# Edge scores of an attention layer: linear term from the value projection, gather in two float32r products, heads halved on POOL, projections first

## The reference

```python
Xq = (H @ W_lin.T).reshape(bt, n, h, dh)
Xv = (H @ W_val.T).reshape(bt, n, h, dh)
Qs, Kt = Xq[:, src], Xq[:, dst]
e = einsum('behd,hd->beh', leaky_relu(Qs + Kt, 0.2), a)
e = e + log(A0[src, dst] + EPS)[None, :, None]
attn = softmax of e over the edges that share src
Y = segment_sum(attn[..., None] * Xv[:, dst], src)
return Y.reshape(bt, n, d) @ W_out.T
```

## Time and profile before

| | |
|---|---|
| median of 3 runs | 1267.29 us (1266.42 to 1267.98) |
| profiled execution | 1267.61 us |
| its span, first to last instruction | 1265.7 us |
| mean granted TensorE clock | 0.995 |
| score stage (turns 0 to 15) | about 992 to 1142 us of the span |

### The profile page before, as it was taken

How to read it: one execution, slowest core, us unless ns; L and a number is a source line. 1 busy time by engine, 2 the same in 40 slices (tenths; PEclk the granted TensorE clock), 3 DMA queues, 4 the chain that set the end, 5 groups by cost and what they waited for, 6 DMA issues and landing times.

```text
span 1265.7 us, 22613 instructions
## 1 busy us (share of the span) xinstructions
PE 1226.4 (97%) x7334; PEld 1021.7 (81%) x7334; DVE 1012.4 (80%) x2032; ACT 871.6 (69%) x1657; POOL 335.3 (26%) x748
## 2 busy tenths in 40 slices
PE   8989989999999998999999999999999899999998
PEld 8989976653588886788879877988898777878998
DVE  6888859977678876988798879887876699987664
ACT  5666658868478877877787778777765577763332
POOL 6777730000176430000000000000000566653331
PEclk9999999999999999999999999999999999999999
DMA  8000000000211100000000000002100300001112
GB/s 310 2 1 2 2 1 0 0 1 0 100 68 66 66 34 1 1 1 1 1 1 1 1 1 1 1 1 84 51 1 1 134 1 1 2 1 47 71 68 83
DMA packets 14923, 38.22 MB, mean 30 GB/s; under 512 B 1904, under 2 KB 3952, under 8 KB 13808
## 3 DMA queue, kind: packets, MB, share of 16 engines
q1 hardware_dynamic: 14000, 36.60, 7.6%
q10 hardware_dynamic: 832, 0.46, 0.1%
HBM read 20.27 MB, written 16.78 MB: 29 GB/s over the span
## 4 chain that ended last, share of the span: by engine, by line
PE 53%; DVE 5%; ACT 2%; issue 1%; POOL 1%; POOLq 0%; DVEq 0%; ACTq 0%
PE bank L1108 7%; PE bank L1110 7%; PE bank L1109 7%; PE bank L1580 4%; PE bank L1123 4%; PE bank L1374 4%; PE bank L1119 4%; PE bank L1120 4%; PE bank L1362 4%; PE bank L1570 2%; PE bank L1588 2%; ACT gates L1138 1%; PE bank L1346 1%; PE bank L1264 1%; DVE Y L1193 1%
## 5 line engine op out<-in xcount | busy, mean ns | idle before, releaser
L1138 ACT ACTIVATE gates<-bank,lstm_bias 128x512 f32<-128x512 f32 (+1 forms) x504 | 301.9, 636 | 100.9 <-PE bank L1123 87.7
L170 ACT ACTIVATE l_h<-X,nmr,rstd 128x128 f32<-128x128 f32 (+1 forms) x512 | 210.0, 483 | 48.0 <-POOLq L164 31.0
L1108 PE MATMUL bank<-lstm_node_hi,Wih_hi 128*128 128x512 f32 (+1 forms) x408 | 149.4, 366 | 0.0
L1110 PE MATMUL bank<-lstm_node_lo,Wih_hi 128*128 128x512 f32 (+1 forms) x408 | 148.9, 365 | 0.0
L1109 PE MATMUL bank<-lstm_node_hi,Wih_lo 128*128 128x512 f32 (+1 forms) x408 | 148.8, 365 | 0.0
L138 POOL TENSOR_TENSOR l2r_sum<-l2r_st 128x8 f32<-128x8 f32 x16 | 4.2, 263 | 528.2 <-DVE l2r_st L112 528.2
L1119 PE MATMUL bank<-lstm_hid_hi,Whh_hi 128*128 128x512 f32 (+1 forms) x288 | 104.1, 361 | 3.9 <-DVE lstm_hid_hi L1198 3.8
L1123 PE MATMUL bank<-lstm_hid_lo,Whh_hi 128*128 128x512 f32 (+1 forms) x288 | 106.9, 371 | 0.0
L1120 PE MATMUL bank<-lstm_hid_hi,Whh_lo 128*128 128x512 f32 (+1 forms) x288 | 103.1, 358 | 0.0
L1143 ACT ACTIVATE gates<-lstm_cell 128x512 f32<-128x512 f32 (+1 forms) x144 | 83.7, 581 | 20.8 <-DVE lstm_cell L1185 20.4
L1110 PEld LDWEIGHTS bank<-lstm_node_lo,Wih_hi 128*128 128x128 f32 x408 | 77.1, 189 | 11.6
(11 more groups left out here) (248 smaller groups left out, 3301.7 us busy)
## 6 DMA issues: line engine op xcount, KB each, us to landing
x_spill<-X SPq DMA_DIRECT2D x32, 256.0 KB, 2.0
X<-x_spill SPq DMA_DIRECT2D x2, 4096.0 KB, 12.5
out<-X SPq DMA_DIRECT2D x32, 256.0 KB, 2.0
X<-in_x SPq DMA_DIRECT2D x6, 1024.0 KB, 15.3
X<-in_x SPq DMA_DIRECT2D x3, 512.0 KB, 8.1
w_raw<-in_WihT SPq DMA_DIRECT2D x1, 1024.0 KB, 5.5
w_raw<-in_WhhT SPq DMA_DIRECT2D x1, 1024.0 KB, 7.9
X<-in_x SPq DMA_DIRECT2D x2, 256.0 KB, 3.2
```

What stands on the lines that cost most here:

```text
L170: last = act.activation(h[:, j, :], k.X[:, bass.ds(b0, TB), :][:, j, :], ACT.Relu, bias=k.nmr[:, bass.ds(b0, TB)][:, j:j + 1], scale=k.rst ...
L1108: pe.matmul(out, hi, x_high, start=True, stop=False)
L1110: last = pe.matmul(out, hi, x_low, start=False, stop=it.step == 0)
L1138: act.activation(gate_of(it, g), k.bank[4 * s + g][:, 0:it.N], ACT.Tanh if g == GATE_G else ACT.Sigmoid, bias=k.lstm_bias[:, it.p - 1, g:g ...
```

## The change

- The linear term comes with the value projection. In the output stage of the second layer DVE builds `Wval`, 132 columns (in the place of the weights W1T, which are done with): the 128 of the value projection and four with the query weights times a_sign, summed by head. The value product of a tile then has 132 columns, and ACT copies the last four to `q_sums`. Qs, its POOL product and its DVE sum go.
- The gather is done with F32R operands: ACT rounds the queries to `q_hi`, DVE makes `q_lo = psQ - q_hi`, and PE adds two products for each half. `PT` becomes F32R.
- POOL `halve` adds the upper 16 features of each head in M to the lower 16, in place; DVE `sum_heads` sums those 16, and does so a turn later, behind the additions to X.
- PE does the query products of both slots first, then the value products of both. ACT does `normalise` of turn i+1, slot 0, ahead of the copies q_hi, and that of slot 1 at the end of its turn. DVE's statistics come behind q_lo.
- The PSUM banks are dealt out anew: a tile's values take two banks, one of them that of psT.

```diff
+            def value_projection():
+                W, H = e.Wval[:, :], k.HEADS
+                dve.tensor_tensor(W[:, 0:P], e.Wqv[:, 0:P], e.a_sign[:, :], ALU.mult).then_inc(joined, 1)
+                dve.wait_ge(joined, 1)
+                dve.tensor_reduce(W[:, P:P + H], W[:, 0:P].rearrange("p (x d) -> p x d", x=H), mybir.AxisListType.X,
+                                  ALU.add).then_inc(joined, 1)
+                dve.wait_ge(joined, 2)
+                dve.tensor_copy(W[:, 0:P], e.Wqv[:, P:2 * P]).then_inc(joined, 1)
+
             coef_dve(dve)
+            value_projection()
...
-        self.psR, self.psT, self.psQ, self.psV = (k.bank[n:n + 2] for n in (0, 2, 4, 6))
+        self.psR, self.psT, self.psQ, self.psV = ((k.bank[m], k.bank[n]) for m, n in ((0, 1), (3, 7), (4, 5), (2, 6)))
+        self.values = each(S, lambda s: k.psum[:, (2 + 4 * s) * TW:(4 + 4 * s) * TW].rearrange("p (b x) -> p b x", b=TB))
...
+    def halve(self, pool, i, s):
+        pool.wait_ge(self.R["M"][s], i + 1)
+        heads = self.M[s][:, :, :].rearrange("p c (x d) -> p (c x) d", d=self.k.DH)
+        first, second = heads[:, :, 0:self.k.DH // 2], heads[:, :, self.k.DH // 2:]
+        pool.tensor_tensor(out=first, in0=first, in1=second, op=ALU.add).then_inc(self.R["half"][s], 1)
+
+    def sum_heads(self, dve, i):
+        HW = TB * self.k.HEADS
+        for s in range(self.S):
+            t = i * self.S + s
+            dve.wait_ge(self.R["half"][s], i + 1)
+            dve.tensor_reduce(self.scores[:, :, t * HW:(t + 1) * HW],
+                              self.M[s][:, :, :].rearrange("p c (x d) -> p c x d", x=HW)[:, :, :, 0:self.k.DH // 2],
+                              mybir.AxisListType.X, ALU.add).then_inc(self.R["kept"][s], 1)
...
 on_pool
             for s in range(S):
-                if i:
-                    pool.wait_ge(R["lin"][s], i)
-                pool.wait_ge(R["Xq"][s], i + 1)
-                pool.tensor_tensor(out=Qs[s][:, :, :], in0=Xq[s][:, :, :],
-                                   in1=e.a_sign[:, :].unsqueeze(1).broadcast_to([P, TB, P]),
-                                   op=ALU.mult).then_inc(R["Qs"][s], 1)
+                self.halve(pool, i, s)
             if i + AHEAD < n_it:
                 ln.coefficients(pool, i + AHEAD)
...
 on_scalar
+            if i + 1 < n_it:
+                self.normalise(act, i + 1, 0)
             for s in range(S):
-                if i:
-                    act.wait_ge(R["Qs"][s], i)
                 act.wait_ge(R["Q"][s], i + 1)
-                act.activation(Xq[s][:, :, :], as_tile(psQ[s]), ACT.Copy).then_inc(R["Xq"][s], 1)
+                act.activation(q_hi[s][:, :, :], as_tile(psQ[s]), ACT.Copy).then_inc(R["hi"][s], 1)
+            for s in range(S):
+                t = i * S + s
                 act.wait_ge(R["V"][s], i + 1)
-                act.activation(Xv[:, rows(i, s), :], as_tile(psV[s]), ACT.Copy).then_inc(R["Xv"][s], 1)
-                if i + 1 < n_it:
-                    self.normalise(act, i + 1, s)
+                act.activation(Xv[:, rows(i, s), :], self.values[s][:, :, 0:P], ACT.Copy)
+                act.activation(e.q_sums[:, t * HW:(t + 1) * HW].rearrange("p (b x) -> p b x", b=TB),
+                               self.values[s][:, :, P:P + HEADS], ACT.Copy).then_inc(R["Xv"][s], 1)
+            if i + 1 < n_it:
+                self.normalise(act, i + 1, 1)
...
 on_tensor
-                for n, (ps, done) in enumerate(((psQ[s], R["Q"][s]), (psV[s], R["V"][s]))):
-                    for j in range(TB):
-                        last = pe.matmul(ps[:, j * P:(j + 1) * P], hT[s][:, j, :], e.Wqv[:, n * P:(n + 1) * P],
-                                         start=True, stop=True)
-                    last.then_inc(done, 1)
+                for j in range(TB):
+                    last = pe.matmul(psQ[s][:, j * P:(j + 1) * P], hT[s][:, j, :], e.Wqv[:, 0:P], start=True, stop=True)
+                last.then_inc(R["Q"][s], 1)
+            for s in range(S):
+                for j in range(TB):
+                    last = pe.matmul(self.values[s][:, j, 0:P + HEADS], hT[s][:, j, :], e.Wval[:, :], start=True, stop=True)
+                last.then_inc(R["V"][s], 1)
...
-                for c, (ps, free) in enumerate(((psQ[s], R["Xq"][s]), (psV[s], R["Xv"][s]))):
-                    pe.wait_ge(free, i + 1)
-                    pe.matmul(ps[:, :], e.PT[:, c * P:(c + 1) * P], Xq[s][:, :, :], start=True, stop=True).then_inc(R["G"][s], 1)
+                pe.wait_ge(R["lo"][s], i + 1)
+                for c, ps in enumerate((psQ[s], psV[s])):
+                    if c == 1:
+                        pe.wait_ge(R["Xv"][s], i + 1)
+                    pe.matmul(ps[:, :], e.PT[:, c * P:(c + 1) * P], q_hi[s][:, :, :], start=True, stop=False)
+                    pe.matmul(ps[:, :], e.PT[:, c * P:(c + 1) * P], q_lo[s][:, :, :], start=False, stop=True).then_inc(R["G"][s], 1)
...
 on_vector
             if i + AHEAD < n_it:
-                self.update(dve, i + AHEAD, tail_in)
+                self.add_residual(dve, i + AHEAD, tail_in)
+            if i:
+                self.sum_heads(dve, i - 1)
+            for s in range(S):
+                dve.wait_ge(R["hi"][s], i + 1)
+                dve.tensor_tensor(q_lo[s][:, :, :], as_tile(psQ[s]), q_hi[s][:, :, :].bitcast(F32),
+                                  ALU.subtract).then_inc(R["lo"][s], 1)
+            if i + AHEAD < n_it:
+                self.statistics(dve, i + AHEAD)
...
-            for s in range(S):
-                dve.wait_ge(R["M"][s], i + 1)
-                dve.tensor_reduce(scores[:, :, t * HW:(t + 1) * HW], M[s][:, :, :].rearrange("p c (x d) -> p c x d", x=HW),
-                                  mybir.AxisListType.X, ALU.add).then_inc(R["kept"][s], 1)
-            for s in range(S):
-                dve.wait_ge(R["Qs"][s], i + 1)
-                dve.tensor_reduce(e.q_sums[:, t * HW:(t + 1) * HW], Qs[s][:, :, :].rearrange("p b (x d) -> p (b x) d", x=HEADS),
-                                  mybir.AxisListType.X, ALU.add).then_inc(R["lin"][s], 1)
+        self.sum_heads(dve, n_it - 1)
...
-        self.psV, self.psY, self.psO = ((bank[2], bank[3]), (bank[4], bank[6])), (bank[0], bank[5]), bank[7]
+        self.psV, self.psY, self.psO = ((bank[3], bank[7]), (bank[4], bank[2])), (bank[0], bank[5]), bank[6]
```

More of the change, by code:

```diff
@@ L1239, in __init__ @@
         EC = k.E // P
-        at = lambda name, shape, offset: k.nc.alloc_sbuf_tensor_at(name, shape, F32, offset=offset)
+        at = lambda name, shape, offset, t=F32: k.nc.alloc_sbuf_tensor_at(name, shape, t, offset=offset)
         tile = 4 * TW
-        self.h, self.hT, self.Xq, self.Qs = (each(S, lambda s: at(f"l3_{n}{s}", [P, TB, P], x_at + (m * S + s) * tile))
-                                             for m, n in enumerate(("h", "hT", "Xq", "Qs")))
+        self.h, self.hT = (each(S, lambda s: at(f"l3_{n}{s}", [P, TB, P], x_at + (m * S + s) * tile))
+                           for m, n in enumerate(("h", "hT")))
+        self.q_hi, self.q_lo = (each(S, lambda s: at(f"l3_{n}{s}", [P, TB, P], x_at + (m * S + s) * tile, F32R))
+                                for m, n in ((2, "q_hi"), (3, "q_lo")))
         e.q_sums = at("q_sums", [P, k.B * k.HEADS], w_at)
@@ L1267, in update, with add_residual @@
     def update(self, dve, i, tail_in):
+        self.add_residual(dve, i, tail_in)
+        self.statistics(dve, i)
+    def add_residual(self, dve, i, tail_in):
         X, R = self.k.X, self.R
@@ L1274, in update, with statistics @@
             dve.tensor_tensor(xt, as_tile(self.psR[s]), xt, ALU.add).then_inc(R["updated"][s], 1)
+    def statistics(self, dve, i):
         for s in range(self.S):
-            dve.wait_ge(R["updated"][s], i + 1)
-            self.ln.stats(dve, X[:, self.rows(i, s), :], s, i)
+            dve.wait_ge(self.R["updated"][s], i + 1)
+            self.ln.stats(dve, self.k.X[:, self.rows(i, s), :], s, i)
+    def halve(self, pool, i, s):
[11 more added lines that the diff above has]
+                              mybir.AxisListType.X, ALU.add).then_inc(self.R["kept"][s], 1)
     def normalise(self, act, i, s):
@@ L1285, in on_pool @@
         EC, HEADS, HW = k.E // P, k.HEADS, TB * k.HEADS
-        h, hT, Xq, Qs, M, ln, rows = self.h, self.hT, self.Xq, self.Qs, self.M, self.ln, self.rows
+        h, hT, q_hi, q_lo, M, ln, rows = self.h, self.hT, self.q_hi, self.q_lo, self.M, self.ln, self.rows
         psT, psQ, psV = self.psT, self.psQ, self.psV
@@ L1354, in on_tensor @@
             for s in range(S):
-                if i == n_it - 1 and s == S - 1:
-                    at.sm.turn_back(pe, 0)
                 pe.wait_ge(R["hT"][s], i + 1)
@@ L1455, in linear_term @@
         for c in range(self.EC):
-            last = pe.matmul(self.first[:, c * P:(c + 1) * P], self.e.PT[:, c * P:(c + 1) * P],
+            last = pe.matmul(self.first[:, c * P:(c + 1) * P], self.e.PT[:, c * P:(c + 1) * P].bitcast(F32),
```

18 lines of the change are left out of this document (11 added, 7 removed).

## The result

1331.4 us (median of 5, 1331.2 to 1333.4) against 1268.0 for the kernel before on the same chip (median of 5, 1266.4 to 1269.4): 1.050 times the time [1.049, 1.052], 5% slower. Forecast was 1333, with 1318 to 1350 around it from its own terms and 1316 to 1352 with the rivals taken in. The profiled execution took 1331.8 with a span of 1330.1, 64.4 more than the span of before, so it accounts for the whole difference.

A forecast was written before the change was run, and what follows sets the result against it. PE and DVE were both taken as full at 8.79 us a turn before; after, a loop of waits. Terms 2.8 + 58.1 + 4.8 - 1.0 + 1.3 = 66 on 1267.3 gave 1333 us, range 1316 to 1352.

The forecast's parts named there:

- The closed loop M - halving - coefficients - normalise - q_hi - q_lo - M: Score stage, once a turn: the queue orders make each engine wait for the next, 13.26 us against 8.79, 4.47 more.
- neither waits for the other: Score stage of the kernel before: PE and DVE both fill the 8.79 us turn without waiting for each other.
- turn 0: First turn of the score stage: normalisation stands in front of q_hi, so its last M ends 2.8 us later.
- turn 14: Score stage: no statistics, but the linear-term addition, two transposes and a gather; about 13.4 us for 8.62, 4.8 later.
- turn 15: Last turn of the score stage: normalises nothing; softmax, reductions and q_lo take 4.63 us where 5.59 stood, 1.0 earlier.
- behind E(15): After the end of turn 15's last M: POOL's v_lo queues behind the last halving, delaying PE's gather; 1.3 us later.
- W: Output stage: three new DVE instructions, at most 1.2 us, counted as nothing, with 1.2 kept for the range.
- Busy time (a): Rival, score stage: no waiting, DVE's 7.74 us a turn decides, about 1252 us, faster; 5 in 100.
- The clock (b): Rival, score stage: PE idles, then gathers and projections run slow, 14.6 us a turn, about 1351 us; 8 in 100.
- The rule that the prediction took from the Trainium skill: A loop leaving PE idle long each round starts its products slow; here every turn's gathers would begin at 1.2 GHz.
- The halving (c): Rival, POOL in the score stage: halvings cost 2.5 us each, both on the path, 2.4 a turn, about 1366; 5 in 100.
- (d): Rival, score stage: some links of the path overlap and the stage loses little; 2 in 100.

The follow-up runs named there:

- the kernel with three turns of lead: Kernel after with X, its statistics and its coefficients made three turns ahead instead of two, all queue orders kept: 1251.8 us, ratio 0.987.
- the experiment with late statistics: Kernel after with DVE's statistics of turn i+2 moved behind the products M of turn i: 1334.1 us, ratio 1.052.
- the filled kernel: Kernel after with 16 products without a use added on PE in each turn, behind the value projections: 1332.1 us, ratio 1.051.
- the kernel with the late normalisation: Kernel after with normalise of turn i+1, slot 0, put back on ACT behind the copies of q: 1265.2 us, ratio 0.997.

## Why the prediction was right

**The step that decided it.** The closed loop M - halving - coefficients - normalise - q_hi - q_lo - M was forecast at 13.26 us a turn and measured at 13.01. Link by link, from the turn shown:

| link | forecast | after |
|---|---|---|
| second halving, start to the first coefficient | 1.22 | 1.24 |
| coefficients to normalise (POOL 1062.58, ACT 1066.85) | 4.17 + 0.09 | 4.27 |
| normalise, start to q_hi | 1.56 | 1.55 |
| q_hi to q_lo | 0.70 | 0.61 |
| q_lo, two | 1.20 | 1.21 |
| statistics | 1.55 | 1.55 |
| M, first start to halving of slot 1 | 2.69 + 0.08 | 2.59 |

Nearly all of the 0.25 between them lies in the four M (0.18 less) and in the wake-up of q_lo (0.09 less). The M were sized by a row in which they were not at full pace. In the kernel before they start at 1046.98, 1047.57, 1048.20 and 1048.98; unhindered they are 0.60 apart, so the last one came 0.18 late, with DVE idle for 0.09 ahead of it, too short to be shown. The gathers of that turn run beside them (1045.34 to 1048.78), so a wait for the last gather is the likely reason; that was not tried. It qualifies the reading "neither waits for the other". The busy time of the loop without waits comes to 7.51 (the kernel with three turns of lead), not to 7.74, nearly all of it for the same reason.

**The sum.**

| term | forecast | after |
|---|---|---|
| ahead of the stage | 0 | 0.95 |
| turn 0, E(0) 1005.74 to 1009.19, less the 0.95 | 2.8 | 2.5 |
| turns 1 to 13 (169.11 for 114.21) | 58.1 | 54.9 |
| turn 14 (14.26 for 8.62) | 4.8 | 5.6 |
| turn 15 (12.80 for 13.01) | -1.0 | -0.2 |
| behind E(15) (124.74 for 124.12) | 1.3 | 0.6 |
| sum | 66 | 64.4 |

The four ends, from the timeline of DVE in the kernel after: the last M of turns 0, 13, 14 and 15, against the earlier trace rows.

```profile
1006.72 2.47 DVE L1452 SCALAR_TENSOR_TENSOR l_M<-psum,a_sign 128x512 f32<-128x512 f32 x4
...
1175.80 2.50 DVE L1452 SCALAR_TENSOR_TENSOR l_M<-psum,a_sign 128x512 f32<-128x512 f32 x4
...
1191.08 1.48 DVE L1452 SCALAR_TENSOR_TENSOR l_M<-psum,a_sign 128x512 f32<-128x512 f32 x2 [0.23 <-PE psum L1419]
...
1204.08 1.28 DVE L1452 SCALAR_TENSOR_TENSOR l_M<-psum,a_sign 128x512 f32<-128x512 f32 x2
```

- Turn 14 has no statistics to cover PE, and its M waited on gathers at a granted clock of 0.50, 1.71 for the first and the 0.23 above for the second slot, as in the experiment with late statistics. From the first M to the last it is 3.19 where the other turns have 2.47. Hence 0.8 more than forecast.
- Turn 15 gave back less than forecast. Its path goes through the softmax pieces on DVE, and one of them took 1.54 where it takes 0.69 (last section). The forecast also has a slip of 0.1 here: 5.59 less 3.44 leaves 2.15 of softmax, not 2.25.
- The 0.95 ahead of the stage is no effect of the change. It came up in the first layer, where both kernels leave PE idle for the 3.19 of the earlier trace rows: from 169.56 on the kernel after stayed longer on the slow clock behind it. No instruction of the change runs there. Among the ten kernels of the experiments the first coefficients of the stage end between 1.6 us before (the kernel before with the early normalisation) and 2.3 us behind (three turns of lead) those of the kernel before, with the same work ahead of them or all but the same: it is the scatter of single executions. What makes the clock differ there was not tried.
- W cost nothing: its three instructions on DVE take 0.87 (271.50 to 272.37), and the offset between the two kernels is 0.96 ahead of them (DVE 257.64 for 256.68) and 0.95 behind them, at 281.

**The rivals.** Busy time (a) did not decide. But what it named, some 15 us from a loop bound by DVE, is close to what three turns of lead gave: 16. So the saving was real, and was spent on the wait. That the two numbers are so close is in part luck: turns 1 to 13 gave 17.8 (7.41 on average for 8.79), and turn 0, which has one more turn to prepare, took about 2.6 back. The clock (b): PE does idle each turn and its gathers do run at 1.2 GHz (0.42 to 0.43 from start to start, a granted clock of 0.55 and 0.58 in the windows that hold them), and it costs nothing, as the filled kernel shows. Only the size of the cover was luck: take the statistics away and it is 14.6 us. The rule that the prediction took from the Trainium skill, page "TensorE: Matmul & The Clock Gate", section "HAM oscillation — how this bites in real kernels", is borne out in a loop, but not in every turn: behind 2.8 to 4.6 us of idling in turns 1 to 14, the gathers began slow in eight of the fourteen (0.57 to 0.60 from the first product to the second); in the other six the first products came at 0.23 to 0.41 and only the later ones at 0.43. Whether the slow products are on the path is a question of its own, and here they are not. The projections were not slow as a whole (1.00 from 1063 to 1069), so PE's turn never came to 14.6. The halving (c) takes 1.29 in place and in runs of 16 elements (its mean on the page is 1287 ns), the same as any 512 elements: the dear one did not come about. (d) did not either: no link overlapped.

**The signs.** Turn 13.0 for 13.3; ACT idle 3.27 before the normalisation, by POOL; DVE idle 3.70 in the turn shown, 4.6 on average (59.8 in 13) before q_lo, by ACT; the halving released by M and the coefficients behind it. Only PE was busier than "little over half", 70 to 75%, and idled 3.7 a turn ahead of the gathers (47.7 in 13) for the 5.8 forecast. The forecast had its work at the fast clock; in the turn before the one shown the gathers took 3.58 (1056.74 to 1060.32) for 1.9 and the transposes 2.91 for 1.77, while the projections took 3.76, as forecast.

## What to carry to other kernels

Where every engine works in order and hands work around, look for the closed path before adding up busy times: start at an operation, ask what stands ahead of each instruction in its queue, and see whether you come back within one turn. Two moves can close such a path that do little alone (the early normalisation by itself 4 us, all the rest of the change without it 3 us less than the kernel before, both together 63 more), and one more turn of lead can cost next to nothing and divide its length by the number of turns that it then spans: 1331 became 1252 by one digit. And work that seems to lengthen the path may be the cover of something slower: move it away only together with what it hid.

## What the runs showed of the hardware that was not expected

- **A scan on DVE waits for POOL.** In turn 15 a halving on POOL and a scan with two inputs from SBUF ran into each other, in the timeline of the kernel after:

```profile
1192.63 1.28 POOL L1307 TENSOR_TENSOR l_M<-l_M 128x512 f32<-128x512 f32 x1 [0.42 <-DVE l_M L1452]
...
1192.92 1.54 DVE L1520 TENSOR_TENSOR_SCAN sm_m<-reset,sm_r 128x256 f32<-128x256 f32 x1
...
1194.49 0.69 DVE L1524 TENSOR_TENSOR_SCAN sm_w<-reset,sm_m 128x256 f32<-128x256 f32 x1
```

The first scan was held until about when POOL was done (1193.91) and shows its wait as busy time, 1.54 for 0.69; the second, alone, takes 0.69, as both do in the kernel before. The same scan takes 0.69 in the kernel without the halving and 1.53 to 1.74 in all eight kernels with it. The Trainium skill, page "SBUF — State Buffer", section "SBUF: two separate sides", says that DVE and GpSimd share a pair of ports that only one holds at a time, and that a DVE operation with two SBUF inputs needs it against a GpSimd operation that reads SBUF. With this the trace agrees. The products M, with one input from PSUM, did not slow down beside POOL's first halving: four take 2.47 to 2.50, and 2.47 in the kernel without the halving.

- **Products of 512 columns in float32r**: 0.23 to 0.24 from start to start at the fast clock (the gathers of the kernel with the late normalisation), 0.42 to 0.43 at 1.2 GHz (the gathers behind PE's idle time in the kernel after).
- **The same code, at another clock.** The 0.95 us of the first layer: behind the same 3.19 of idle time the granted clock was 0.50 from 169 to 175 in the execution of the kernel after, and in that of the kernel before 1.00 until 170, 0.50 only from 171 to 173 and 1.00 again from 174 on.
